# A selective-scan kernel on one core: the convolution lump in two pieces, two buffers for the normalized input, the bias by TensorE and a single sigmoid pass

## The reference

```python
xn = _layernorm(x)
xz = einsum('ed,bld->bel', in_proj_w, xn)          # x half and z half
def _mamba_dir(xz, ...):                            # forward, and again on reversed tokens
    u = silu(causal_conv(x, conv_w) + conv_bias)    # 4 taps
    x_dbl = einsum('bdl,kd->bkl', u, xproj_w)       # 8 rows for delta, 16 B, 16 C
    delta = softplus(dtproj_w @ x_dbl[:r] + dt_bias)
    h = scan(exp(delta * A), delta * B * u)         # 16 states for each of 256 channels
    y = sum_n(h * C) + Dp * u
    return y * silu(z)
x + out_proj(out_f + out_b) + (quantize(xn @ H) @ ternary(weight).T)
```

## Time and profile before

| | |
|---|---|
| median of 3 runs | 818.29 us (816.92 to 818.44) |
| the profiled execution's own time | 815.69 us |
| its span, first to last instruction | 813.9 us |
| VectorE busy | 738.6 us (91%), 800 instructions |
| ScalarE busy | 740.7 us (91%), 1423 instructions |
| TensorE busy (products) | 727.0 us (89%), 3921 instructions |
| GpSimd busy | 698.0 us (86%), 339 instructions |
| mean granted TensorE clock | 0.973 |

### The profile page before, as it was taken

The page is one execution under the profiler, slowest core; times in us unless marked ns, Lnnn a source line. Parts: engine busy times, 40 slices in busy tenths (PEclk is TensorE's granted clock), DMA queues, the critical chain, the costliest instruction groups (busy, mean ns, idle before and its releaser), DMA issues. The chain is left out here.

```text
span 813.9 us, 11948 instructions
## 1 busy us (share of the span) xinstructions
PE 727.0 (89%) x3921; PEld 376.6 (46%) x3921; DVE 738.6 (91%) x800; ACT 740.7 (91%) x1423; POOL 698.0 (86%) x339
## 2 busy tenths in 40 slices
PE   7877999889998899989999899998999889998995
PEld 5435354353634436353453536444363444635363
DVE  4667899989999899998999989998999989999996
ACT  3699999999999999999989999899999999899890
POOL 0288789897998979899898979989798997989995
PEclk9798999999999999999999999999999999999698
DMA  6547072441806136070631608144180804417000
GB/s 198 147 118 144 1 170 54 104 95 41 173 24 162 37 86 151 26 173 1 150 88 59 140 4 194 40 116 82 57 180 4 188 7 119 106 42 155 2 14 26
DMA packets 55117, 74.80 MB, mean 92 GB/s; under 512 B 6784, under 2 KB 23568, under 8 KB 55056
## 3 DMA queue, kind: packets, MB, share of 16 engines
q1 hardware_dynamic: 54624, 73.79, 38.8%
q10 hardware_dynamic: 432, 0.26, 0.1%
HBM read 62.49 MB, written 11.53 MB: 91 GB/s over the span
## 5 line engine op out<-in xcount | busy, mean ns | idle before, releaser
L697 POOL TENSOR_TENSOR hst<-hst,c_rep 128x1024 f32<-128x1024 f32 x255 | 596.5, 2369 | 71.6 <-DVE hst L593 54.8
L593 DVE TENSOR_TENSOR_SCAN hst<-da,b_ps 128x512 f32<-128x512 f32 x512 | 580.4, 1198 | 28.9 <-issue 13.8
L408 ACT ACTIVATE da<-rep,neg_a 128x511 f32<-128x511 f32 x504 | 330.7, 709 | 3.5 <-DVE hst L593 3.1
L395 ACT ACTIVATE dbx_t<-du_t,b_t 128x256 f32<-128x256 f32 x640 | 274.1, 496 | 4.7 <-PE b_ps L910 4.0
L910 PE MATMUL b_ps<-ident,dbx_t 128*128 128x128 f32 x1536 | 224.0, 284 | 55.7 <-DVE hst L593 37.8
L910 PEld LDWEIGHTS b_ps<-ident,dbx_t 128*128 128x128 f32 x1536 | 173.1, 144 | 161.0 <-DVE hst L593 87.8
L933 PE MATMUL y<-hst,sum_sel 128*32 128x512 f32 x1024 | 138.9, 616 | 0.0
L814 PE MATMUL pb<-xnt,conv_wt 128*128 128x512 f32 x240 | 110.5, 603 | 13.8 <-ACT du_t L378 13.0
L888 PE MATMUL b_ps<-du,spread_sel 32*128 32x512 f32 x256 | 89.4, 669 | 0.5 <-DVE hst L593 0.4
L582 DVE TENSOR_TENSOR b_ps<-b_ps,b_rep 128x1024 f32<-128x1024 f32 x64 | 77.8, 1218 | 9.5 <-PE b_ps L888 6.0
L814 PEld LDWEIGHTS pb<-xnt,conv_wt 128*128 128x128 f32 x240 | 43.1, 189 | 80.8 <-issue 61.1
(11 more groups left out here) (120 smaller groups left out, 457.4 us busy)
## 6 DMA issues: line engine op xcount, KB each, us to landing
rep<-d_scr SPq DMA_DIRECT2D x128, 256.0 KB, 9.5
c_rep<-bc_scr SPq DMA_DIRECT2D x64, 256.0 KB, 4.9
d_scr<-t_pos SPq DMA_DIRECT2D x16, 512.0 KB, 3.0
b_rep<-bc_scr SPq DMA_DIRECT2D x64, 64.0 KB, 2.3
x_ln<-x SPq DMA_DIRECT2D x8, 256.0 KB, 3.8
x_res<-x SPq DMA_DIRECT2D x8, 256.0 KB, 3.1
out<-x_res SPq DMA_DIRECT2D x8, 256.0 KB, 2.3
rep<-x SPq DMA_DIRECT2D x7, 256.0 KB, 4.7
```

The source lines that it names most:

```text
L395: ins = nc.scalar.activation(dbx_t[(NX * d + q - 1) % 2][:, c, :, r, :], du_t[d][:, c, :, :], ACT.Copy, scale=b_t[d][:, c, n:n + 1])
L408: nc.scalar.activation(da[s % 2][:, j, 1:L], rep[d][h][:, j, 1:L], ACT.Exp, scale=neg_a[:, d, h, j, q:q + 1]).then_inc(decay_done, 1)
L593: nc.vector.tensor_tensor_scan(hst[s % RING][:, j, :], da[s % 2][:, j, :], b_ps[:, j, :], 0.0, ALU.mult, ALU.add).then_inc(scan_done, 1)
L697: nc.gpsimd.tensor_tensor(hst[s % RING][:, two, :], hst[s % RING][:, two, :], c_rep[d][:, q:q + 1, :].broadcast_to([P, 2, L]), ALU.mult).t ...
```

## The change

1. The bias. `conv` begins with a product of `bias_w` (row 0 holds the bias of both directions, the other 127 rows are 0) by `ones` (128 x 512), and the taps are added to it. There is a new transfer for the bias row and new memsets for `bias_w` and `ones`; TensorE waits for these before its first transposes.
2. The sigmoid. `t_exp` is left as tanh; `make_u` computes (t + 1) * convolution, which is twice `u`. The factor 2 is taken back in `xproj`, `skip`, the copy of the transposed `du`, and `spread_sel`. Since the step replicas also go through `spread_sel`, each of their eight products is issued twice and accumulated.
3. `xnt` has two buffers that alternate by batch; `xnt_kept` and its copy are gone.
4. The order of work. The forward unit's convolution of half 0, which stood in one piece behind slot 5, is put in two pieces into slot 6. The output projection of the batch before is issued in one lump in slot 4 of the backward unit. In slot 0 of the backward unit ScalarE copies the second half of `du_t` ahead of the sigmoid.

The core of the diff (declarations, buffer indices and changed counts are left out):

```diff
             def u_sigmoid(d, V, h):
-                nc.scalar.activation(t_exp[:, h, :], source, ACT.Tanh, bias=half_bias[:, d, h:h + 1], scale=0.5).then_inc(u_step, 1)
-                act.wait_ge(u_step, 2 * V + h + 1)
-                nc.scalar.activation(t_exp[:, h, :], t_exp[:, h, :], ACT.Copy, bias=0.5, scale=0.5).then_inc(u_sig, 1)
+                nc.scalar.activation(t_exp[:, h, :], source, ACT.Tanh, scale=0.5).then_inc(u_sig, 1)
...
             def make_u(d, V, h):
-                nc.vector.scalar_tensor_tensor(u[d][:, h, :], source, col[:, d, 0, h:h + 1], t_exp[:, h, :], ALU.add, ALU.mult).then_inc(u_ready, 1)
+                nc.vector.scalar_tensor_tensor(u[d][:, h, :], t_exp[:, h, :], 1.0, source, ALU.add, ALU.mult).then_inc(u_ready, 1)
...
             def keep_xnt(b):
-                wait(act, kept_ready, b)
-                nc.scalar.activation(xnt[:, PAD:PAD + L], pb[:, 0, :], ACT.Copy).then_inc(xnt_ready, 1)
+                wait(act, had_filled, b - 1)
+                nc.scalar.activation(xnt[b % 2][:, PAD:PAD + L], pb[:, 0, :], ACT.Copy).then_inc(xnt_ready, 1)
...
                     if s == 0:
+                        if d == 1:
+                            keep_dut(d, U, 1)
...
-                        if d == 1 or not first(b):
+                        if d == 0 and not first(b):
                             keep_dut(d, U, 1)
...
             def conv(d, V, h, taps, free, count):
+                if 0 in taps:
+                    mm(bank, bias_w[:, d, P * h:P * (h + 1)], ones[:, :], start=True, stop=False)
...
             def step_replicas(h, js):
-                    mm(pb[:, j % 2, :], spread_sel[at, :], t_pos[at, h, :], start=True, stop=True).then_inc(rep_filled, 1)
+                    mm(pb[:, j % 2, :], spread_sel[at, :], t_pos[at, h, :], start=True, stop=False)
+                    mm(pb[:, j % 2, :], spread_sel[at, :], t_pos[at, h, :], start=False, stop=True).then_inc(rep_filled, 1)
```

More of the change, by code:

```diff
@@ L33, with build @@
 SKIP_AT = 3
-def build(nc, x, win_t, wz_t, conv_w, cols, xproj_t, dt_t, a_log, wout_t, ffn_w, had, ident_d, sum_sel_d, spread_d, out):
+def build(nc, x, win_t, wz_t, conv_w, bias_rows, cols, xproj_t, dt_t, a_log, wout_t, ffn_w, had, ident_d, sum_sel_d, spread_d, out):
     ctx = ExitStack()
@@ L67, in build @@
         shift = sb("shift", [P, NB * NC])
-        xnt = sb("xnt", [P, PAD + L + PAD])
-        xnt_kept = sb("xnt_kept", [P, L])
+        xnt = [sb(f"xnt{n}", [P, PAD + L + PAD]) for n in range(2)]
         amax = sb("amax", [P, NC])
@@ L483, in unit @@
                         inputs_t(d, U, 3, 3)
[L484 to L487, removed]
+                        if d == 0 and not last(b):
+                            keep_xnt(b + 1)
                     if s == 6 and d == 0:
@@ L614, in _ @@
             dve.wait_ge(w_loaded, DMA * W_LOADS)
-            nc.vector.tensor_scalar(half_bias[:, :, :], col[:, :, 0, :], 0.5, None, ALU.mult).then_inc(weights_ready, 1)
+            for d in range(2):
+                nc.vector.tensor_scalar(xproj[d][:, :, :, :], xproj[d][:, :, :, :], 0.5, None, ALU.mult).then_inc(weights_ready, 1)
             dve.wait_ge(ident_loaded, DMA)
@@ L753, in _ @@
             pool.wait_ge(const_ready, 3)
+            nc.gpsimd.memset(bias_w[:, :, :], 0.0).then_inc(zeroed, 1)
+            nc.gpsimd.memset(ones[:, :], 1.0).then_inc(ones_ready, 1)
             for d in range(2):
@@ L756, in _ @@
                 nc.gpsimd.memset(dtw[d][:, :], 0.0).then_inc(zeroed, 1)
-            for d in range(2):
-                nc.gpsimd.memset(xnt[:, d * (PAD + L):d * (PAD + L) + PAD], 0.0).then_inc(zeroed, 1)
+            for n in range(2):
+                for d in range(2):
+                    nc.gpsimd.memset(xnt[n][:, d * (PAD + L):d * (PAD + L) + PAD], 0.0).then_inc(zeroed, 1)
             pool.wait_ge(first_delta, 1)
@@ L1005, in unit @@
                             transpose_xq(b, xq_ready, b + 1)
-                        elif last(b):
-                            du_transposed(V, 1, gate_ready, 2 * b + 1)
-                        else:
-                            du_transposed(V, 1, xnt_ready, b + 2)
+                        elif not last(b):
+                            pe.wait_ge(xnt_ready, b + 2)
+                            conv(0, U + 2, 0, range(2), dut_ready, 2 * V + 1)
                     if s == 7 and not last(b):
@@ L1023, in unit @@
                         transpose_xn(b + 1, gate_ready, 2 * b + 1)
-                    if s == 4 and d == 1 and not first(b):
-                        project(b - 1, (2, 3), xqt_ready, b)
                     if s == 5 and d == 1 and nxt:
@@ L1030, in unit @@
                             du_transposed(V, 0, out_ready, b)
+                    if s == 6 and d == 0:
+                        if last(b):
+                            du_transposed(V, 1, gate_ready, 2 * b + 1)
+                        else:
+                            du_transposed(V, 1, xnt_ready, b + 2)
+                            conv(0, U + 2, 0, range(2, TAPS), dut_ready, 2 * V + 1)
                     if s == 6 and d == 1 and nxt:
@@ L1036, in unit @@
                             skip_products(b, d)
-                        if s == 5 and not last(b):
-                            if d == 0:
-                                pe.wait_ge(xnt_ready, b + 2)
+                        if s == 5 and d == 1 and not last(b):
                             conv(d, U + 2, 0, range(TAPS), dut_ready, 2 * V + 1)
```

43 lines of the change are left out of this document (22 added, 21 removed).

## The result

The changed kernel takes 807.59 us (median of 4 runs, 806.4 to 808.76). The kernel before, on the same chip, takes 817.61 us (4 runs, 816.77 to 818.44). The ratio is 0.9886 [0.987, 0.9903]: 10.0 us less, where 4.8 were forecast. The profiled execution took 806.40 us with a span of 804.6, against 815.69 and 813.9, so 9.3 us less.

What follows compares the result with a forecast made beforehand. It took VectorE's scans to set the pace, with TensorE's row limiting the forward-to-backward boundary. Start +6.0 us and steady part -10.8 us sum to -4.8 us, so 818.29 becomes 813.5 us; range 805.5 to 819.0.

Steps and rivals of the forecast that it cites:

- the forecast's own 810 to 817: Main case, chance 0.55, at 813.5 us: start costs 2.5 to 8 us, steady part wins 9 to 11.
- rival (a): Start: TensorE's clock stays at 2.4 GHz, so the start costs 1.2 us instead of 6.0; 808.7 us, chance 0.20.
- (b): Forward-to-backward boundary gives nothing because TensorE's row is 0.7 us longer than added up; 818.6 us, chance 0.13.
- (c): Bias products have no cover at TensorE's three unsplit lumps, each batch 1.3 us longer; 828.1 us, chance 0.12.
- The first batch was to be about 5 us longer: Sign expected in the profile after: first batch about 5 us longer than before, first `x_proj` near 22.7 us.
- Forward to backward unit: At this boundary, multiplication by B starts 0.69 us sooner and second `u` comes sooner; 0.93 us won per batch, seven times.
- Projection: Output projection in one lump lets the backward unit's residual start sooner; 0.86 us won, six times.
- Backward to forward: Unsplit convolution with bias makes the forward unit's second `u` 0.21 us later, less 0.08; 0.13 us lost, seven times.
- Steady sum: Steady part: 7 x 0.93 + 6 x 0.86 - 7 x 0.13 = 10.8 us won.
- Bias products before the first `x_proj`: Start: three bias products (2.6 us) come before the first `x_proj`, which had waited 0.49 us; 2.1 us later.
- the term of 3.9 us for the doubled replicas: Start: each step replica product issued twice at 1.2 GHz makes each decay pair 1.7 us later; 3.9 us lost.
- 2.3 pairs: Start: of three decay pairs, 2.3 were taken to run at 1.2 GHz, the clock falling somewhat after the first begins.

Runs made afterwards that it cites:

- the lump put back: Changed kernel with the forward unit's convolution of half 0 in one piece behind slot 5 again; 808.88 us, ratio 0.9909.
- the three others with the same start: Changed kernel with, one at a time, the split convolution back in one piece (808.88 us), the projection in halves (812.63), the `du_t` copy behind the decays (810.52).
- the last version above: Changed kernel with the bias product as bf16 rows in all but the first three convolutions and step replicas issued once; 791.44 us, ratio 0.9695.
- The one trace that was taken for this: Changed kernel run once more, unedited, beside other runs of before; median 807.11 us, ratio 0.9895, profiled execution a long one with a span of 1415.9 us.

## Why the prediction was wrong in size

The direction was right, and so was the shape of the steady part. The forecast of the change, -4.8 us, was about half of what was measured. The measured time lies in the range of all cases, 805.5 to 819.0, but 2.4 us below the forecast's own 810 to 817. It is nearest to rival (a), 808.7, which had a chance of 0.20, and that nearness is in part luck: (a) had the start at 1.2 us and the steady part at 10.8, where the trace shows 2.5 and 11.7. Rivals (b) and (c) fall with the batches, 1.64 us shorter each. The first batch was to be about 5 us longer; unit 1's first scan came 1.63 us later.

- *Forward to backward unit, 0.93 us.* Right. The gaps of 0.55 and 1.97 us went, and 1.95 us came before the multiplication by B (said: about 1.8) and 0.95 before `u` (said: 1.2). The claim that TensorE's row and not the lump's place holds the boundary is shown by the lump put back: 0.20 us a batch.
- *Projection, 0.86 us.* Right: 0.80 by the kernel with the halves, and 0.18 us of wait left (said: 0.19).
- *Backward to forward, -0.13 us.* The wait is 0.65 (said: 0.6), and slot 5 shows no new gap, as was said. What it left out are the two waits of 0.17 us before each unit's last multiplication by B, which the kernel before does not have and which are gone when the bias products are left out.
- *Steady sum, 10.8 us.* Measured 11.66 (0.73 + 10.93). A batch agrees. The 0.9 us more is 0.46 in units 1 and 2 (94.61 to 93.35, forecast 0.80), 0.26 in the batch behind them (96.21 to 94.29, forecast 1.66) and 0.27 in the last unit, for which the sum had no term, less 0.1 in the rest.
- *Bias products before the first `x_proj`, 2.1 us.* 1.75 measured, and 1.75 to 2.16 in the three others with the same start.
- *The step that failed is the term of 3.9 us for the doubled replicas*, and in it the "2.3 pairs" at 1.2 GHz, not the 1.7 us each. In the profiled execution no pair saw that clock, and the term was 0.73 us. In the three others with the same start it was 2.1 to 2.9 us, with the last pair partly at 1.2 GHz. The row that I trusted, TensorE busy for 9.11 of 10 us at 1.2 GHz, is of a sequence whose clock had fallen at 29.8, with single products. The doubled ones kept 2.4 GHz until 34.8 to 39.1 us in seven traces; the single ones lost it at 28.2 to 33.4 us in four. Rival (a) was this mechanism. Its price (1.2 us) was too low, though. It had the doubled pairs keep pace with the old ones at 1.2 GHz, which all but the first do: the kernel before still ran its first pair at 2.4 GHz, in 1.89 us (27.69 to 29.58), where the doubled one takes 2.76, so 0.87 us is lost there (lines below). And it had the transposes and copies behind the replicas win 0.9 us at 2.4 GHz, but the clock fell at 39.1 us, just ahead of them; 0.24 us was won.

The first pair of decays and the start of the next in the kernel before, and TensorE's stretch with one replica each, ahead of the fall at 33.4 us:

```profile
27.69 1.26 ACT L373 ACTIVATE da<-pb,neg_a 128x511 f32<-128x511 f32 x2
29.58 1.44 ACT L373 ACTIVATE da<-pb,neg_a 128x511 f32<-128x511 f32 x2 [0.63 <-PE pb L895]
```

```profile
31.40:33.30 1.90, 1.90 (x10) 0.97 (x7) 1.90 (x2) 1.26 (x2) 0.39 (x2) 1.00 1.04 207
```

Of the 5.2 us between forecast and measurement, the profiles account for 4.5: 3.2 at the replicas, 0.35 at the bias, 0.1 between slots 1 and 2, 0.9 in the steady part. How much of the 3.2 an execution gets depends on when its clock falls: 1.0 to 1.8 in the three dearer starts. The rest lies between the medians and the profiled executions.

The Trainium skill ("TensorE: Matmul & The Clock Gate", HAM oscillation) says that a busy array keeps the high clock and that idle gaps bring the low one. The traces agree in direction: with doubled replicas the fall came at 34.8 to 39.1 us, with single ones at 28.2 to 33.4, and my doubt of it was wrong. They also show why the busy share misled me: from 30 to 36 us TensorE is busy for 5.80 us at a clock of 1.00 with doubled replicas (the kernel before with them), and for 5.84 us at 0.52 with single ones (the last version above). At 1.2 GHz each product lasts longer, so that the low clock itself makes the row look full.

What stays open: why the clock falls at all where it does. Ahead of the fall at 29.8 us in the kernel before, TensorE was busy 1.55 of 1.90 us (27.7 to 29.6), but with one replica each it was busy all of 1.90 us (31.4 to 33.3) and the clock fell at 33.4, with no idle gap to explain it. Open too is why the same instructions keep the clock until 36.7 us in one execution and until 39.1 in another, each kernel having one usable trace, and whether the median execution has the early or the late fall. The one trace that was taken for this gave no answer.

## What to carry to other kernels

A gap on the bottleneck engine is worth only what the engine that feeds it can come sooner: add up that engine's row up to the next thing that is waited for, idle time included, before counting a gap as won. A row of a slow-clock stretch prices the sequence that was running there; if the edit changes how densely that stretch is filled, price it at both clocks, since the busy share of a slow stretch is raised by the slow clock. And when an operation is moved to the matrix engine for its spare time, its type is a price of its own: the same bias holds up the taps by 0.86 to 0.97 us as fp32 and by 0.23 as split bf16 rows.

## What the hardware showed that I had not expected

- Two products in the same 32 rows of the array, against one: a pair of decays every 2.75 us instead of 1.90 at 2.4 GHz, and, by the estimate above, 4.6 instead of 2.84 at 1.2 GHz. Twice the products at 2.4 GHz took a little less time than single ones at 1.2.
- A bf16 product can open an accumulation in PSUM that fp32 products continue, and it costs its own 0.23 us there.
- `scalar_tensor_tensor` for `u` takes 683 ns in place of 747. The edit put a number in place of the column and also made the PSUM operand the second tensor instead of the first; which of the two saves the 64 ns no run shows.
